# Values convolved by four accumulating TensorE products of shifted tokens, key tiles ahead of query tiles

## The reference

```python
q = silu(_causal_depthwise_conv(h @ Wq, conv_q))      # 768 channels
k = silu(_causal_depthwise_conv(h @ Wk, conv_k))      # 768 channels
v = silu(_causal_depthwise_conv(h @ Wv, conv_v))      # 1536 channels
# conv: out[t, c] = sum over j in 0..3 of (h @ W)[t - 3 + j, c] * w[c, j], zeros ahead of t = 0
gk = -exp(A_log) * softplus(h @ Wgk + dt_bias);  beta = sigmoid(h @ Wb + b_b)
def step(S, inp):                                     # a scan over the 512 tokens
    S = S * exp(gt);  delta = (vt - kt @ S) * bt
    S = S + outer(kt, delta);  return S, qt @ S
```

## Time and profile before

| | |
|---|---|
| median of 3 runs | 3829.35 us (3812.28 to 3831.82) |
| span of the profiled execution, first to last instruction | 3803.2 us |
| PE busy | 3028.9 us (80%) |
| DVE busy | 1929.8 us (51%) |
| ACT busy | 1619.0 us (43%) |
| POOL busy | 801.2 us (21%) |
| ahead of the first score product (L500) | 130.9 us |
| one row | 459.3 us (L1139 starts at 274.7 us first and at 3489.8 us last, seven rows apart) |

### The profile page before, as it was taken

The page is one execution under the profiler, slowest core; times in us unless marked ns, Lnnn a source line. Parts: engine busy times, 40 slices in busy tenths (PEclk is TensorE's granted clock), DMA queues, the critical chain, the costliest instruction groups (busy, mean ns, idle before and its releaser), DMA issues.

```text
span 3803.2 us, 61240 instructions
## 1 busy us (share of the span) xinstructions
PE 3028.9 (80%) x21188; PEld 2136.8 (56%) x21188; DVE 1929.8 (51%) x4785; ACT 1619.0 (43%) x3753; POOL 801.2 (21%) x517
## 2 busy tenths in 40 slices
PE   1587987779787896879869799787987879887896
PEld 1255763467544674447744477354773557634685
DVE  3237643566435664356552665427653376435663
ACT  0137442464325543265423654237442374424643
POOL 0004310133103321033210432004310043102331
PEclk7688987889888997889978899788987889878897
DMA  3300012000210003001030000300003000120002
GB/s 93 66 3 13 13 23 60 3 14 14 44 38 4 15 12 79 4 3 16 9 80 4 6 15 8 80 4 9 14 16 70 3 13 13 26 58 3 14 14 37
DMA packets 228391, 96.33 MB, mean 25 GB/s; under 512 B 176114, under 2 KB 218236, under 8 KB 225668
## 3 DMA queue, kind: packets, MB, share of 16 engines
q1 hardware_dynamic: 223826, 89.88, 11.9%
q10 hardware_dynamic: 4224, 2.10, 0.2%
HBM read 70.74 MB, written 21.17 MB: 24 GB/s over the span
## 4 chain that ended last, share of the span: by engine, by line
PE 56%; ACT 15%; issue 10%; DVE 8%; DMA 5%; SPq 4%; POOL 1%; DVEq 0%; ACTq 0%; POOLq 0%
PE bank L540 7%; DMA vq<-qk_bounce 3%; PE bank L792 3%; SPq L1738 3%; PE bank L593 3%; PE bank L602 3%; PE bank L854 2%; PE bank L825 2%; PE bank L772 2%; PE bank L716 2%; PE bank L804 2%; PE bank L774 2%; PE bank L776 2%; PE bank L794 2%; PE bank L500 2%
## 5 line engine op out<-in xcount | busy, mean ns | idle before, releaser
L1658 POOL TENSOR_TENSOR arena<-upto,gk 128x1536 f32<-128x1536 f32 x32 | 88.1, 2753 | 1540.9 <-DVE beta L1139 1540.9
L500 PE MATMUL bank<-vq 72*128 72x128 bf16 (+3 forms) x512 | 189.8, 435 | 176.6 <-DMA vq<-qk_bounce 158.2
L1146 DVE SCALAR_TENSOR_TENSOR arena<-bank,conv,arena 128x510 f32<-128x510 f32 (+1 forms) x384 | 285.5, 747 | 72.8 <-ACT arena L1436 50.0
L540 PE MATMUL bank<-arena,vq 128*32 128x512 f32 (+3 forms) x1024 | 302.8, 446 | 0.0
L1036 DVE TENSOR_REDUCE mx<-bank 128x1 f32<-128x128 f32 (+3 forms) x512 | 217.0, 482 | 166.3 <-PE bank L501 162.6
L1650 POOL TENSOR_TENSOR arena<-arena 128x511 f32<-128x511 f32 x192 | 243.3, 1269 | 222.0 <-DVE arena L1146 221.9
L1401 ACT ACTIVATE arena<-bank 128x384 f32<-128x384 f32 (+1 forms) x384 | 175.8, 528 | 240.0 <-PE bank L527 240.0
L664 PE MATMUL bank<-h_t,arena 128*128 128x512 f32 x384 | 225.3, 682 | 51.3 <-DVE arena L1146 51.2
L1523 ACT COPY u<-bank 32x128 f32<-32x128 f32 x192 | 49.3, 257 | 470.9 <-PE bank L786 469.8
L500 PEld LDWEIGHTS bank<-vq 72*128 72x128 bf16 x512 | 64.9, 128 | 263.8 <-issue 174.9
L716 PE MATMUL bank<-vq 64*128 64x128 f32 x1536 | 166.6, 314 | 52.8 <-ACT arena L1510 36.5
(11 more groups left out here) (294 smaller groups left out, 7094.1 us busy)
## 6 DMA issues: line engine op xcount, KB each, us to landing
vq<-qk_bounce SPq DMA_DIRECT2D x162, 128.0 KB
arena<-w_bounce SPq DMA_DIRECT2D x16, 1024.0 KB, 16.4
qk_bounce<-arena SPq DMA_DIRECT2D x18, 384.0 KB, 2.4
arena<-in_L_attn_Wv_dram SPq DMA_DIRECT2D x8, 768.0 KB, 20.3
t<-t_bounce SPq DMA_DIRECT2D x256, 12.0 KB, 1.7
x<-t_bounce SPq DMA_DIRECT2D x256, 12.0 KB, 1.7
arena<-in_L_attn_Wq_dram SPq DMA_DIRECT2D x8, 384.0 KB, 15.1
arena<-in_L_attn_Wk_dram SPq DMA_DIRECT2D x8, 384.0 KB, 17.7
```

The costliest lines, as they stand in the source:

```text
L500: mm(ps[:, 0:e], q_stack[0:KS, h, t * P:e], k_stack[0:KS, h, 0:e], start=True, stop=False)
L540: last = mm(y_bank(g)[r:r + 32, j * P:T], v32[:, j, h, :], p_t[:, h % 2, c0:c0 + n], start=(j == 0), stop=(j == NT - 1))
L1146: ins = V.scalar_tensor_tensor(a[:, k:T], ps[:, 0:T - k], conv[:, n, 3 - k:4 - k], a[:, k:T], ALU.mult, ALU.add)
```

## The change

Queries and keys keep their path, with the key tiles (6 to 11) ahead of the query tiles (0 to 5): `TILES`. So `keys(0)` needs only the first six Silus.

The values leave that path. Ahead of the loop Wv and the taps are loaded as constants (the taps copied to all partitions), POOL multiplies them to three tiles `wv_made` of 128 x (4 taps x 512 channels), and SP writes these to DRAM (`wv_bounce`, 1 MB each). In each row SP reads them back, the first with the other weights at the row's start, the other two behind the experts (`moe_ps`).

The values' convolution is then 12 units (3 groups of 4 heads x 4 chunks of tokens), each of four products of 128x128 by 128x512 that accumulate in one bank, with the tokens, shifted by 3, 2, 1 and 0, as the stationary operand. `h_t` gets four zero columns in front (`h_pad`) for the shift. The result is in token layout, and one Silu on ACT writes it into `v_all`. The 12 transposing steps, the copies, and the values' taps on ACT, DVE and POOL are gone. Units 0 to 3 stand between the tiles of `conv(0)`, 4 and 5 behind `gram(0)`, 6 and 7 behind `attend(0)`, 8 behind `mask(1)`, 9 to 11 behind `attend(1)`; `levels(0)` waits for all 12 Silus.

```diff
-        acc = arena[:, 8 * HW:8 * HW + 4 * T].rearrange("p (i t) -> p i t", i=4)
+        acc = arena[:, 7 * HW:7 * HW + 4 * T].rearrange("p (i t) -> p i t", i=4)
+        VG = GH * DV
+        v_at = [2 * HW, 7 * HW + 4 * T, 7 * HW + 4 * T + 4 * VG]
+        wv = [arena[:, o:o + 4 * VG].rearrange("p (k v) -> p k v", k=4) for o in v_at]
...
+        def v_bank_of(u):
+            return PS[6 + u % 2] if u < V_FIRST else PS[2 + u % 3]
...
             if c == 0:
-                stages += [("values", 1), ("scale_v", 0)]
+                stages.append(("scale_v", 0))
...
-        act_stops = [NQK + 1, NQK + 5, NQK + 9, NCV]
-        pe_stops = [NQK + 1, NQK + 2, NQK + 5, NQK + 9, NCV]
-        tap_stops = [NQK + 4, NQK + 8, NCV]
-        add_stops = [NQK + 4, NCV]
+        V_FIRST = 4
+        TILES = list(range(NP, NQK)) + list(range(NP))
+        V_UNITS = [(g, c) for g in range(NG) for c in range(NT)]
+        V_AFTER = {3: 0, 5: 1, 7: 2, 9: 3}
...
-        pe_stages = ([("conv", 0)] + first[1:4] + [("conv", 1)] + first[4:] + [("conv", 2)] + second
-                     + [("conv", 3), ("values", 0), ("gram", 1), ("attend", 1), ("conv", 4)] + stages)
-        act_stages = [("conv", 0)] + first + [("conv", 1)] + second + [("conv", 2), ("conv", 3)] + stages
+        pe_stages = ([("conv", 0)] + first[1:4] + vals(4, 5) + first[4:] + vals(6, 7) + second + vals(8)
+                     + [("gram", 1), ("attend", 1)] + vals(9, 10, 11) + stages)
+        act_stages = ([("conv", 0)] + first + silu_on + vals(4, 5, 6, 7) + silu_off + second + silu_on
+                      + vals(8, 9, 10, 11) + silu_off + stages)
...
+            (wv_raw, L1_attn_Wv),
         ]
+        const_loads += [(taps_of[g], L1_attn_conv_v[g * VG:(g + 1) * VG, :].rearrange("c k -> (c k)").partition_broadcast(P))
+                        for g in range(NG)]
...
+                def convolve_v(u):
+
+                    g, c = V_UNITS[u]
+                    if c == 0:
+                        pe.wait_ge(wv_in[g], at(b, wv_in[g], 16))
+                    if u >= V_FIRST + 3:
+                        pe.wait_ge(v_tok, at(b, v_tok, u - 2))
+                    elif u >= V_FIRST:
+                        pe.wait_ge(taps, at(b, taps, NQK))
+                    elif u >= 2:
+                        pe.wait_ge(v_tok, at(b, v_tok, u - 1))
+                    ps = v_bank_of(u)
+                    for k in range(4):
+                        t0 = c * P + 1 + k
+                        last = mm(ps[:, :], h_pad[:, t0:t0 + P], wv[g][:, k, :], start=(k == 0), stop=(k == 3))
+                    last.then_inc(v_conv_ps, 1)
...
                 def convolve(i):
+                    for m, n in enumerate(TILES):
+                        if m == Z_LEAD:
                             decays()
+                        elif m == 2 * Z_LEAD:
                             mask(0)
+                        if m in V_AFTER:
+                            convolve_v(V_AFTER[m])
+                        if m >= 3:
+                            pe.wait_ge(taps, at(b, taps, m - 2))
+                        mm(z_bank(m)[:, :], wconv[:, n * P:(n + 1) * P], h_t, start=True, stop=True).then_inc(z_ps, 1)
...
                     if c == 0:
-                        pe.wait_ge(taps, at(b, taps, NCV))
+                        pe.wait_ge(taps, at(b, taps, NQK))
+                        pe.wait_ge(v_tok, at(b, v_tok, HD))
...
+                def silu_v(u):
+                    g, c = V_UNITS[u]
+                    act.wait_ge(v_conv_ps, at(b, v_conv_ps, u + 1))
+                    A.activation(v_all[:, c, GH * g:GH * (g + 1), :].rearrange("p h v -> p (h v)"), v_bank_of(u)[:, :],
+                                 ACT.Silu).then_inc(v_tok, 1)
...
                 def convolve(i):
+                    for m in range(Z_LEAD):
+                        first_tap(m)
+                    decays()
+                    silu_set(1)
+                    for m in range(NQK):
+                        silu(m)
+                        if m + Z_LEAD < NQK:
+                            first_tap(m + Z_LEAD)
+                        if m + Z_LEAD in V_AFTER:
+                            silu_v(V_AFTER[m + Z_LEAD])
+                    silu_set(0)
...
+            pool.wait_ge(consts_in, CONSTS)
+            for g in range(NG):
+                G.tensor_tensor(wv_made[g].rearrange("p (k v) -> p k v", k=4), taps_of[g].rearrange("p (v k) -> p k v", k=4),
+                                wv_raw[:, g * VG:(g + 1) * VG].unsqueeze(1).to_broadcast([P, 4, VG]), ALU.mult).then_inc(wv_scaled, 1)
+            pool.wait_ge(wv_scaled, NG)
...
+            for g in range(NG):
+                sp.wait_ge(wv_scaled, g + 1)
+                sp.dma_start(wv_bounce[g], wv_made[g]).then_inc(weights_out, 16)
             sp.wait_ge(rows_out, 16)
             sp.wait_ge(out_sent, 16)
-            sp.wait_ge(weights_out, 32)
+            sp.wait_ge(weights_out, 80)
...
-                sp.dma_start(wconv[:, 2 * nq:2 * nq + nv], L1_attn_Wv).then_inc(wc_in, 16)
+                sp.dma_start(wv[0].rearrange("p k v -> p (k v)"), wv_bounce[0]).then_inc(wv_in[0], 16)
...
                 tokens(b, 1)
+                sp.wait_ge(moe_ps, at(b, moe_ps, NE))
+                for g in range(1, NG):
+                    sp.dma_start(wv[g].rearrange("p k v -> p (k v)"), wv_bounce[g]).then_inc(wv_in[g], 16)
```

More of the change, by code:

```diff
@@ L107, in adaln_two_layers @@
         router1 = sb("router1", [P, NE])
-        conv = sb("conv", [P, NCV, 4])
+        conv = sb("conv", [P, NQK, 4])
         bqk = sb("bqk", [P, 2])
@@ L876, in project @@
                     last.then_inc(wo_ps, 1)
-                walk = {"conv": convolve, "values": values, "keys": keys, "queries": queries, "mask": mask, "gram": gram, "attend": attend,
+                walk = {"conv": convolve, "vals": convolve_v, "keys": keys, "queries": queries, "mask": mask, "gram": gram, "attend": attend,
                         "levels": levels, "project": project,
@@ L935, in _ @@
             then(V.tensor_scalar(wo[:, :, :], wo[:, :, :], gnorm[:, 0:1], None, ALU.mult))
+            V.memset(h_pad[:, 0:4], 0.0)
             V.memset(t16[:, :, :], 0.0)
@@ L1646, in convolve @@
                 def convolve(i):
-                    for n in lots(add_stops)[i]:
-                        pool.wait_ge(taps, at(b, taps, n + 1))
-                        G.tensor_tensor(acc[:, n % 4, 1:T], acc[:, n % 4, 1:T], acc2[:, n % 3, 0:T - 1], ALU.add).then_inc(taps_added, 1)
+                    for m in range(NQK):
+                        pool.wait_ge(taps, at(b, taps, m + 1))
+                        G.tensor_tensor(acc[:, m % 4, 1:T], acc[:, m % 4, 1:T], acc2[:, m % 3, 0:T - 1], ALU.add).then_inc(taps_added, 1)
                 def mask(c):
```

138 lines of the change are left out of this document (52 added, 86 removed).

## The result

| | before | after |
|---|---|---|
| median, runs of the same chips | 3821.32 us (3812.28 to 3831.82, 4 runs) | 3960.99 us (3949.0 to 3967.7, 4 runs) |
| span of the profiled execution | 3803.2 us | 3962.1 us |
| PE busy | 3028.9 us (80%) | 3213.5 us (81%) |
| one row, mean of the last seven | 459.3 us | 475.4 us |
| first score product | 130.9 us | 160.2 us |

The ratio is 1.0391, 95% interval 1.0360 to 1.0422: the change makes the kernel slower by 3.9% by this ratio. Between the two medians of the table it is 140 us, 3.7%, which lies inside that interval. The forecast was +94 us. The time is in the range and the sign is right, but the sum is too small: a row of +7 to +12 us, which had 62%, isn't what came.

The account below looks back on a forecast made before the run. ACT was taken to pace the convolution, neither PE nor ACT full behind it; PE's net 23.9 us a row exceeds 22.4 idle. Eight rows +74 and prologue +20 on 3829.35 give 3923 us, range 3870 to 3975.

Parts of the forecast that it names:

- The unit's price: A value unit of four products on PE takes 3.43 us, bounds 3.2 to 4 us.
- rival (d): Value products overlap so well that a unit takes 2.1 us: -5.4 us a row, 3806 us; chance 2%.
- Step 1: conv(0), now bound by PE, with ACT's tail late: gram(0) starts 7.0 us later, PE idles 9 us ahead of it.
- The reason given for the keys' order: Having keys first doesn't help: gram(0) waits for the mask's exponentials, behind all of conv(0) on ACT.
- Step 2: gram(0) to levels(0): 52.8 us against 47.5, +5.3 us, with 1.2 GHz for 7.7 us behind the idle.
- Step 3: Behind levels(0): values(1) goes, so keys(2) starts sooner, -3.3 us, plus 0.2 for transposes at the lower clock.
- Nothing else of the row is touched: Rest of the row, behind keys(2): no change; the values are ready long before POOL scales them.
- A row: Sum of the row's terms: +9.2 us, eight rows +74 us; a row of +7 to +12 had 62%.
- Step 4: Ahead of the loop: constants 11 us, writes 9 us, POOL's multiplications beside DVE's work; +20 us once, bounds 14 and 30.
- (a): Milder: dense units keep PE at 2.4 GHz, ACT's tail partly overlapped; +4.5 us a row, 3885 us; chance 16%.
- (c): PE's idle and slow time in both rewritten stretches fills up: -10.5 us a row, 3765 us; chance 5%.
- (b): Steeper: clock stays low behind the longer idle, gram(0) to unit 7; +15 us a row, 4045 us, half 3984; chance 12%.

Follow-up runs that it names:

- mask_early: Kernel after, with mask(0) on PE and its exponentials on ACT moved behind the decays, ahead of conv(0)'s Silus; 3932.3 us, ratio 1.0302 to before.
- queries_first: Kernel after, with the tile order undone: query tiles first, then key tiles, keys(0) waiting for all twelve Silus; 3966.58 us, ratio 1.0405 to before.
- unit8_subst: Kernel after, with unit 8 right behind keys(1) on PE and subst(0) ahead of the sums of squares on DVE; 3900.66 us, ratio 1.0266 to before.
- one_product: Kernel after, with only one of the four products of each value unit, to price the products; 3794.04 us, ratio 0.9942 to before.
- moves_two: Kernel after, with mask(0) behind the decays, unit 8 behind keys(1), unit 9 ahead of attend(1), prologue fills first; 3868.82 us, ratio 1.0161 to before.
- memsets_after: Kernel after, with DVE's prologue fills ahead of its first wait instead of behind its scalings; 3947.32 us, ratio 1.0350 to before.
- memsets_before: Kernel before, with DVE's prologue fills ahead of its first wait, nothing else; 3799.62 us over 12 runs, ratio 0.9952 to before.

## Why the prediction was right or wrong

**The unit's price: right.** 3.43 us, 0.86 a product, as the earlier trace rows had it. The section "Back-to-back issue gap" of "TensorE: Matmul & The Clock Gate" in the Trainium skill, as the prediction works it out, would have given 2.1 us, an estimate; the trace doesn't agree, and rival (d) falls with it.

**Step 1: right.** +7.0 forecast, +7.2 measured (32.6 to 39.9). The idle of about 9 us is 8.86, and PE has no wait for DVE between its products. The mask's exponentials behind all of conv(0) on ACT were the cause: mask_early takes 6.6 us back. The reason given for the keys' order holds too (queries_first).

**Step 2: right in kind, too small.** levels(0) comes 53.9 us behind gram(0) in six of seven rows, 52.8 forecast. (The sum has a slip: 38.6 + 1.9 + 0.9 is 41.4, not 41.7, so its own terms give 52.5.) The row that the forecast was read from has 47.5 us; the mean of seven before is 46.8. What the terms had wrong is mask(1). They took its 3.2 us at full clock from conv(0), though the earlier trace rows has its first product at 2.05 us, against 1.02 in conv(0). Nor are the rows quite alike. In six of seven rows the clock falls there again, behind waits of 2.43 and 0.72 us (L687 and L720 in the row above), and mask(1) takes 5.0 us. In the seventh, of 59.1 us, it stays full behind the same two waits and falls at attend(1). First the ordinary row at mask(1), then the seventh from gram(0) to levels(0) by stretch, then PE in order of time in it:

```profile
2750.00:2754.00 4.00, 3.51 (x5) 1.43 (x7) 3.27 (x15) 1.92 (x7) 0.00 (x0) 0.57 0.00 0
```
```profile
1293.70:1302.00 8.30, 8.18 (x29) 5.60 (x30) 3.02 (x6) 2.27 (x8) 3.98 (x4) 0.50 0.01 2
1302.00:1334.00 32.00, 26.88 (x110) 14.35 (x110) 13.73 (x40) 13.55 (x26) 3.21 (x2) 0.98 0.05 7
1334.00:1343.00 9.00, 8.74 (x29) 5.73 (x30) 3.42 (x6) 0.00 (x0) 7.18 (x5) 0.50 0.27 40
1343.00:1352.00 9.00, 8.89 (x20) 3.62 (x18) 0.00 (x0) 1.27 (x3) 0.00 (x0) 0.94 0.20 26
```
```profile
1322.78 2.17 PE L720 MATMUL bank<-arena,later 128*128 128x512 f32 x4 [0.72 <-ACT arena L1505]
...
1334.20 4.53 PE L731 MATMUL bank<-vq 64*128 64x128 f32 x24 [2.01 <-DVE bm L1196]
```

1.2 GHz behind the 8.86 us of idle was forecast. A second fall stood only in the bounds, behind the pause ahead of mask(1); it comes there in six rows (some 1.7 us lost), and behind the 2.01 us ahead of attend(1) in the seventh, where PE runs at 0.50 while busy for 8.74 of 9.00 us (some 4.5 us lost). Together the step cost +7.8 us, not +5.3. What attend(1) waits for is DVE, as forecast. The wait is 0.33 us in the six rows, where PE is late itself by the slow mask(1), and 2.01 us where mask(1) runs at full clock; the difference is the 1.7 us. Why the clock falls at one of the two places and not at the other isn't shown.

**Step 3: right.** -3.1 forecast, -2.9 measured.

**"Nothing else of the row is touched": wrong.** From keys(2) to the row's end it is +2.5 us and from there to the first score product +1.5: 4 us a row that no term had. In the first part the instructions are the same and the low clock grew by as much (from 17.3 to 20.5 us a row). Behind levels(1), before and after (PE in order of time; L792 of before is L808 of after):

```profile
410.36 3.85 PE L792 MATMUL bank<-arena,bm 64*128 64x64 f32 x24
```
```profile
452.82 5.09 PE L808 MATMUL bank<-arena,bm 64*128 64x64 f32 x24
```

Where in the later work the clock is low shifts with what went ahead. unit8_subst, with all products, has 200.5 us for this part as before has; it isn't a fixed cost of the change, and one_product, with a quarter of the products, has 202.8, so their amount doesn't make it. In the rows of after this part differs by 2.6 us from one to the next, in those of mask_early by 6.4. The wait for the stacks scatters by far more than 1.5 us from row to row (9.7 to 21.4 us), and nothing here tells a cost from chance.

**A row: +9.2 forecast, +16.1 measured.** By terms +0.2, +2.5, +0.2 and +4.0 too little. That is between two profiled executions, and the one of before was a short one (see the sizes below): by the medians a row is +13.8 us, so some 2 of the 7 us missed are chance of the profile. The steps that failed are "Nothing else of the row is touched" and the full clock for mask(1).

**Step 4: mis-sized, by a step that failed.** +20 forecast. The load of tokens moved by 25.1 us, in six profiles of this prologue 94.2 to 95.7. The constants cost 8.1 us (33.2 to 41.3; 11 forecast), the writes 7.4 (9 forecast; from DVE's last fill to the load 8.3 us became 15.7). What failed is "POOL's three multiplications lie beside DVE's work ... they just fit": their time fits (16.6 us), but they hold DVE for 9.6 us (5.08 + 5.36 instead of 0.18 + 0.68). The Trainium skill, "SBUF — State Buffer", section "SBUF: two separate sides", says that DVE, for instructions in a two-port mode or with two inputs in SBUF, and GpSimd take one pair of ports as an exclusive lock, that whoever starts first has it for the whole instruction, and that the other blocks fully. The trace agrees in that a copy of 128x8 takes 5.08 us and ends with POOL's instruction, while a copy out of PSUM isn't held. The other 4.2 us of the first score product's +29.3 are the landing of the stacks: 43.1 us from the first issue (117.1 to 160.2) against 38.6 before, and 29.8 to 42.2 in the other kernels, so I don't count them to the change.

**The rivals.** (a) and (c) fall as accounts of the kernel as it was built: the clock was low behind the idle, and the idle stayed. But moves_two shows what was true in them: of after's 3.9% over before, 2.3 points were order and the fills of the prologue (the fills alone 0.4, memsets_after), and 1.6 remain, some 7 us a row by the medians for 23 us of products. Against before with the same fills (memsets_before) 1.8% remain. (b) falls in its form (the clock is full again by attend(0), 2.58 us); a second fall is real, but costs 1.7 us in most rows. The measured 3961 lies near the 3984 of half of (b), and by another way: 1.7 to 4.5 us more of clock a row where half of (b) has 7.7, and time in places that (b) doesn't name. That the range held is in part luck: it was wide enough on this side for a case that didn't come.

**The sizes.** Between the profiled spans it is +158.9 us, of which the eight rows hold 8 x 16 = 128 and the prologue 29. The medians differ by 140. A run's time is 1.7 us above its span in after (3963.82 and 3962.1); if that holds for before, its profiled execution took 3804.9 us, 16 us under its median, and that of after lay 3 us above. So by the medians the eight rows hold 140 - 29 = 111 us, 13.8 a row.

## What to carry to other kernels

Work given to an engine with idle time is free only if it lands in that idle time; find for each pause whom it waits for, and move that (here mask(0) on ACT) before counting the pause as room. When one wait goes, the next chain behind it (here DVE's subst(0)) decides, and the same move can help in one order and hurt in another. POOL work "beside" DVE work has to be checked instruction by instruction, in the prologue too. And before a row's difference of 1 to 3 us between two single profiles is explained, the medians of the runs have to show it.

## What the runs showed of the hardware

- A DVE copy of 128x8 took 5.08 us and a scalar_tensor_tensor of 8x512 5.36 us beside POOL multiplications of 5.5 us that read SBUF; 0.17 and 0.68 us without.
- The granted clock was 0.50 in a stretch where PE was busy for 8.74 of 9.00 us, right behind an idle time of 2.0 us; in the rows where that idle time was 0.33 us it was full there, but had fallen 11 us earlier, at mask(1).
- Behind the same two idle times (2.43 and 0.72 us) the clock fell in six rows of one execution and stayed full in one.
- Two executions with the same row code differed by 3 us a row, with 4 us more low clock.
